# State-space rounds: the gates' table visit at a round's first unit, last gate copies half a unit earlier, two step products behind unit 12

## What is computed

```python
for i in range(nl):                                   # 4 layers
    h = _rms(x, norm_w[i])
    xz = jnp.einsum('bld,ed->ble', h, W_in[i])
    xi, z = jnp.split(xz, 2, axis=-1)
    xc = conv_b[i] + sum((xp[:, k:k + L, :] * conv_w[i][:, k] for k in range(dc)))   # xp: xi, padded by 3
    xc = _silu(xc)
    dbc = jnp.einsum('bld,ed->ble', xc, W_x[i])
    delta, Bm, Cm = jnp.split(dbc, [rk, rk + n], axis=-1)
    delta = jax.nn.softplus(jnp.einsum('blr,dr->bld', delta, W_dt[i]) + b_dt[i])
    A = -jnp.exp(A_log[i])
    deltaA = jnp.exp(delta[..., None] * A)
    BX = (delta * xc)[..., None] * Bm[:, :, None, :]
    _, hs = jax.lax.associative_scan(combine, (deltaA, BX), axis=1)
    y = jnp.einsum('bldn,bln->bld', hs, Cm) + D[i] * xc
    out = jnp.einsum('bld,ed->ble', y * _silu(z), W_out[i])
    x = x + out
```

## Time and profile before

| | |
|---|---|
| median of 3 runs | 1266.38 us (1265.89 to 1266.97) |
| the profiled execution | 1270.83 us |
| its span, first to last instruction | 1269.1 us |
| busy: PE, DVE, ACT, POOL | 1101.1, 1027.9, 851.7, 774.7 us |
| mean granted TensorE clock | 0.938 of full speed |
| table loads on ScalarE | 66 of 1283 ns |

### The profile page before, as it was taken

How to read it: one execution, slowest core, us unless ns; L and a number is a source line. 1 busy time by engine, 2 the same in 40 slices (tenths; PEclk the granted TensorE clock), 3 DMA queues, 4 the chain that set the end, 5 groups by cost and what they waited for, 6 DMA issues and landing times.

```text
span 1269.1 us, 19550 instructions
## 1 busy us (share of the span) xinstructions
PE 1101.1 (87%) x6960; PEld 724.8 (57%) x6960; DVE 1027.9 (81%) x1605; ACT 851.7 (67%) x1889; POOL 774.7 (61%) x635
## 2 busy tenths in 40 slices
PE   7798888888849989889989899899998488999886
PEld 3555555444326566565655665666656456666655
DVE  3567777666699999999899999999998885766567
ACT  1455555655477878778688777897686437888854
POOL 5101111100379989899899898998998952554202
PEclk8899999997969999998999999999999789999976
DMA  7000002000420510503305007023051012100000
GB/s 214 13 13 13 12 13 74 2 1 3 146 102 1 213 42 4 206 18 117 138 1 204 22 2 252 1 101 125 1 208 34 1 39 64 34 18 17 2 1 27
DMA packets 22149, 79.26 MB, mean 62 GB/s; under 512 B 4935, under 2 KB 8847, under 8 KB 21138
## 3 DMA queue, kind: packets, MB, share of 16 engines
q1 hardware_dynamic: 22054, 78.02, 18.0%
HBM read 76.77 MB, written 1.24 MB: 61 GB/s over the span
## 4 chain that ended last, share of the span: by engine, by line
PE 29%; DVE 28%; POOL 20%; ACT 13%; issue 8%; DMA 1%; SPq 0%; DVEq 0%; POOLq 0%; ACTq 0%
PE ps L681 25%; POOL arena L2071 12%; DVE ps L2140 10%; POOL arena L2083 5%; ACT L676 4%; DVE arena L2145 4%; PE ps L750 3%; ACT ps L1939 3%; DVE arena L2143 3%; DVE hstat L1220 2%; DVE arena L1196 1%; POOL arena L2060 1%; ACT arena L1905 1%; ACT arena L942 1%; DMA arena<-in_exb 1%
## 5 line engine op out<-in xcount | busy, mean ns | idle before, releaser
L681 PE MATMUL ps<-arena 128*32 128x100 f32 (+12 forms) x3442 | 563.3, 383 | 56.5 <-ACT arena L1905 15.9
L2071 POOL TENSOR_TENSOR arena<-arena 128x1600 f32<-128x1600 f32 x128 | 457.3, 3592 | 18.0 <-DVE ps L2140 9.7
L681 PEld LDWEIGHTS ps<-arena 128*32 128x32 f32 (+9 forms) x3442 | 284.9, 146 | 274.6 <-issue 110.4
L1939 ACT ACTIVATE ps<-arena 128x400 f32<-128x400 f32 x512 | 283.4, 589 | 151.0 <-DVE arena L2143 106.2
L2140 DVE TENSOR_TENSOR_SCAN ps<-ps,arena 128x800 f32<-128x800 f32 x176 | 320.6, 1822 | 21.2 <-ACT ps L1939 13.5
L648 POOL TENSOR_SCALAR stat<-stat 100x1 f32<-100x1 f32 (+1 forms) x43 | 8.4, 196 | 417.8 <-DVE stat L627 417.0
L1625 PE MATMUL ps<-ident,arena 128*100 128x128 f32 x1536 | 194.6, 285 | 34.4 <-POOL arena L2083 32.3
L1625 PEld LDWEIGHTS ps<-ident,arena 128*100 128x100 f32 x1536 | 176.5, 134 | 58.2 <-POOL arena L2083 37.2
L2143 DVE TENSOR_TENSOR arena<-ps,arena 128x800 f32<-128x800 f32 x176 | 174.5, 991 | 6.0
L2083 POOL TENSOR_TENSOR arena<-arena 128x1600 f32<-128x1600 f32 x40 | 143.4, 3585 | 17.5 <-DVE arena L2145 17.5
L2145 DVE TENSOR_TENSOR_SCAN arena<-ps,arena 128x800 f32<-128x800 f32 x80 | 140.4, 1804 | 6.9 <-ACT ps L1939 6.9
(11 more groups left out here) (211 smaller groups left out, 1140.7 us busy)
## 6 DMA issues: line engine op xcount, KB each, us to landing
arena<-bc_scratch SPq DMA_DIRECT2D x64, 800.0 KB, 6.3
arena<-in_ctxT SPq DMA_DIRECT2D x16, 361.0 KB, 4.0
arena<-in_w_in SPq DMA_DIRECT2D x4, 1024.0 KB, 4.9
arena<-in_expT SPq DMA_DIRECT2D x1, 2048.0 KB, 13.0
arena<-in_w_out SPq DMA_DIRECT2D x4, 512.0 KB, 3.5
arena<-in_mask SPq DMA_DIRECT2D x8, 141.0 KB
arena<-in_xT SPq DMA_DIRECT2D x2, 400.0 KB, 4.1
x_tok<-in_x_tok SPq DMA_DIRECT2D x1, 800.0 KB
```

The costliest lines, as they stand in the source:

```text
L681: return nc.tensor.matmul(outp, lhsT, rhs, start=first, stop=last)
L1939: last = nc.scalar.activation(psf[:, half_at(k) + j * GT:half_at(k) + (j + 1) * GT], delta[g][:, c], ACT.Exp, scale=aneg[:, l % 2, n:n + 1])
L2071: nc.gpsimd.tensor_tensor(bx[:, unit % BX].rearrange("p (j t) -> p j t", j=SEGMENT), bbc[:, nq].rearrange("p (j t) -> p j t", j=SEGMENT), ...
```

## The change

ScalarE's visit to the SiLU table for the gates moves from behind the second half of unit 3 to behind the second half of unit 0. The copies of X6 and X7 move from behind the second half of a round's unit 0 to behind the first. TensorE's products for D2 and D3 at unit 14 move from ahead of the sum of unit 12 to behind it. No instruction is added or removed.

```diff
@@ AT
-    "aV": 3.5,
+    "aV": 0.5,
@@ AT
-    "aZ": (15.5, 15.5, 16.5, 16.5),
+    "aZ": (15.5, 15.5, 16.0, 16.0),
@@ mam_pe
                         if u == AT["pY1"]:
                             pm_conv(pe, m + 1, 1)
                             pm_conv(pe, m + 1, 0)
-                        for c in (2, 3):
-                            if u == AT["pD"][c]:
-                                pm_dt(pe, m + 1, c)
                     if UNITS * m + u >= LAG_R:
                         pm_reduce(pe, UNITS * m + u - LAG_R)
                     for c in range(CD - 1):
@@ mam_pe
                     if m + 1 < ROUNDS:
                         if u == AT["pB"]:
                             pm_dbc(pe, m + 1)
-                        for c in (0, 1):
+                        for c in range(CD):
                             if u == AT["pD"][c]:
                                 pm_dt(pe, m + 1, c)
```

## The result

The changed kernel takes 1278.62 us (median of 8 executions, 1269.59 to 1286.21), the kernel before 1266.14 (8 executions, 1261.56 to 1268.16): a ratio of **1.0104**, 95% interval 1.0069 to 1.0139. The profiled one is the quickest of the eight, 1269.59 us with a span of 1267.8, so its span alone doesn't show the loss; its joints do. A joint is the passage from one round to the next, and its time is that of the window from one start of GpSimd's product for unit 1 to the next.

A forecast was written before the change was run, and what follows sets the result against it. Rounds bound by a chain passing between GpSimd, VectorE and ScalarE, with TensorE setting the pace behind unit 15. 1270.83 + 2.45 + 2.1 + 8.5 - 1.7 = 1282.2, carried to the median 1278 us; range 1268 to 1284.

The forecast's parts named there:

- The visit gains nothing: Joints: VectorE's 0.88 us wait at unit 4 goes, its wait for GpSimd at unit 7 grows instead; gain nothing.
- The copies wait for X7: ScalarE at the joint: second copy waits for X7, unit 1's scan 0.35 us later, seven times, 2.45 us.
- Round 0: Stage start: the visit now precedes unit 1's exponentials, making the round 2.1 us longer, once; bounds 1.85 and 4.15.
- The products behind the sum, clock at full speed: TensorE, D2 and D3 behind unit 12's sum: at full clock the swap costs and gives nothing.
- A fall costs 1.70: Unit 12's sum: each drop of TensorE's clock to 1.2 GHz costs 1.70 us, with no cover left.
- the chances: Forecast's list of odds: slower with three to seven falls 0.62; two falls of double length would make 1284 us.
- Five falls of seven: Unit 12's sum: joined idle of 2.4 to 3.3 us drops the clock in five of seven joints, 8.5 us.
- The rule of the Trainium skill: TensorE: bursts separated by waits each begin at the lower clock; all seven joints fall, 3.4 us more.
- the carrying over from the profiled execution to the median: Whole kernel: the median lies 4.45 us below the profiled execution, taking 1282.2 to 1277.7.
- the 1.7 us subtracted for the one long joint of before: The 86.13 us round had a double-length fall costing 1.7 us; new falls take its place.
- Rival 1: Joints: the clock falls no oftener than now, only copies and round 0 cost; 1270.9 us, chance 0.22.
- Rivals 2 and 3: 2: copies don't hold ScalarE up, 1268.5, chance 0.08; 3: VectorE's unit 4 wait is on the path, 1260.1, chance 0.08.

The follow-up runs named there:

- the run with part of the idle filled: The changed kernel with four products of the identity with itself, read by nothing, ahead of unit 12's sum; 1271.85 us, 1.0047 of the kernel before.
- the filled kernel: The changed kernel with ten products of the identity with itself, read by nothing, ahead of unit 12's sum; 1269.87 us, 1.0016 of the kernel before.

## Why the prediction was right

1278 us were predicted, 1278.62 measured. The mechanism holds: the step products behind the sum join two idle stretches, the clock falls oftener, and nothing covers the falls. That the number agrees to 0.6 us is luck: the interval reaches 4.4 us to either side, and the terms, each by itself, are not all of the right size.

- **The visit gains nothing.** Right, and by the cover that was named: GpSimd's input products. The place was off: I let VectorE's wait for GpSimd grow at unit 7; it came at unit 5 (0.91), and unit 7 kept its 0.57. The input product for unit 5 is one of the same unbroken run.
- **The copies wait for X7.** Predicted 0.35 us a joint; the run of visit and copies shows 84.8 against 84.4, 0.4, with a wait of 0.30 for ScalarE at the predicted spot.
- **Round 0.** Predicted 2.1 us (by its own working it should have been 2.23, the later of the two). In the run of visit and copies GpSimd is 1.83 late, as worked out (1.85); but in the profile of the changed kernel it isn't late at all. What I took as fixed is not: there ScalarE's wait for X7, ahead of the visit, is 2.54 us, where it is 4.78 in the run of visit and copies and in the profile of before. The visit costs only as much as X7 comes late in the stage ahead, and that goes by the clock too: the products that end with X7 take 4.69 us at a granted clock of 0.50 in the profile of before, 2.45 us at 1.00 in that of the changed kernel, whose code is the same there. In the run with part of the idle filled the clock is 0.61, the wait 4.00 and GpSimd 1.19 late. The rows of round 0 (changed kernel; ScalarE, then GpSimd):

```profile
353.88 0.50 ACT L1875 ACTIVATE arena<-ps 128x400 f32<-128x400 f32 x1 [2.54 <-PE ps L681]
```

```profile
364.91 3.57 POOL L2080 TENSOR_TENSOR arena<-arena 128x1600 f32<-128x1600 f32 x1
```

The windows of the products up to X7, before and in the changed kernel:

```profile
355.11:359.80 4.69, 4.69 (x9) 2.40 (x9) 4.33 (x7) 0.00 (x0) 3.71 (x5) 0.50 0.00 0
```

```profile
351.39:353.84 2.45, 2.45 (x9) 1.41 (x9) 2.38 (x4) 0.00 (x0) 2.45 (x1) 1.00 0.00 0
```

- **The products behind the sum, clock at full speed.** Predicted 0; it is 0.2 us a joint (85.0 in the filled kernel and in the changed one, against 84.8 with visit and copies alone). The softplus of D2 waits 0.24 for TensorE, so VectorE's wait at unit 15 grows from 0.24 to 0.65, while the one ahead of its last gating shrinks from 0.83 to 0.65: together 0.23. The prediction had D2 ready at 686.0 and wanted at 685.99, and took that as no wait.
- **A fall costs 1.70.** Measured 86.71 - 85.02 = 1.69 for single length. For double length 87.93 - 85.02 = 2.91, which the sum didn't have (the chances name it). Before, a fall of single length cost 0.1 at most (84.44 and 84.48 us in rounds with a fall, 84.40 without), as the cover of 1.32 us of idle behind the sum has it.
- **Five falls of seven.** The weakest number, from idles of 1.3 and 2.45 us only. The profile of the changed kernel has two, that of the products alone seven. From the medians: 1278.62 less the filled kernel's 1269.87 is 8.75 us. As an estimate from the two prices above, that is five falls if all are of single length and three if all are of double length. So the 8.5 us of the sum came out, but the count of five isn't shown. That executions differ in their falls would account for the spread from 1269.59 to 1286.21. The granted clock of each execution, taken over the whole of it, bears that out in part: it is 0.954 in the quickest of the eight and 0.936 in the slowest, and the four slowest have the four lowest. It doesn't tell in which stage the falls stand, and the executions of before lie 15 us apart as well.
- **The rule of the Trainium skill** (TensorE: Matmul & The Clock Gate, "HAM oscillation"), taken for each round, would have seven falls. The run of the products alone agrees; the changed kernel's profile, with two of seven, does not. The waits of the page's kernel are some 3 to 5 us, those ahead of the sum here 2.47 to 3.38, so as a warning it points the right way, and its count doesn't carry over.

Two sums outside the joints were right only by chance: the carrying over from the profiled execution to the median, and the 1.7 us subtracted for the one long joint of before. The profiles differ by several microseconds in stages that the change doesn't touch.

Rival 1 (no more falls than now, 1270.9) describes the filled kernel, at 1269.87. Rivals 2 and 3 are refuted by the waits of 0.80 and 0.84 on ScalarE and by the run of the visit alone.

## What to carry to other kernels

A wait that the profile lists is worth nothing if the next wait on the same engine is for an engine that runs without a pause behind it: follow the chain to the engine that is released at the joint before counting the gain. When an instruction is moved ahead of another, ask what each of them waits for: putting the one that waits longer first joins the idle stretches, and here the price on TensorE was not the idle but the slower clock behind it, paid by whatever now stood at the back. And look in a queue for work that nobody needs yet standing ahead of a result that an engine already waits for; moving it back cost nothing here and gave half a per cent.

## What was not expected of the hardware

Work that does nothing makes the kernel faster: ten small products a round, with results that nothing reads, take 8.75 us off the median of the changed kernel. What the visit cost in round 0 went by the same clock, in a stage that the change doesn't touch. And the clock is not a function of the length of the idle alone. After 2.46 to 3.38 us of idle ahead of the same sum it fell seven times of seven in one execution (the products alone) and twice of seven in another (the changed kernel); after 0.27 to 1.16 us never in seven, after 1.44 to 2.48 us twice in seven, and of three idles of 2.48 us in that execution two brought a fall and one did not. What decides between two equal idles was not tried.
